# Window attention with an 8x8 Fourier product, then a merge layer: scores ahead of the forward transforms, inverse product ahead of P times V, softmax steps moved forward

## The reference, cut to what matters

```python
# layer 0: x = x + attention(groupnorm(x)), windows of 8x8 = 64 tokens, 6 heads of 32
o = irfft2(rfft2(q * SCALE) * rfft2(k))        # per channel, over the 8x8 window
attn = softmax(o @ v.T + bias)                 # 64 x 64 per window and head
y = attn @ v ;  x = x + y @ proj_w.T + proj_b
# layer 1: x = x + merge(g + laplacian(g)) with g = groupnorm(x)
edges = depthwise 3x3 [[0,-1,0],[-1,4,-1],[0,-1,0]] of g
x = x + 1x1 conv(g + edges, merge_w) + merge_b
```

## Time and profile before

| | before |
|---|---|
| median of 3 | 5582.83 us (5579.11 to 5585.63) |
| profiled execution | 5583.07 us, of which the span is 5581.1 us |
| granted TensorE clock, mean | 0.993 |
| PE busy | 5361.9 us (96%) |
| PEld busy | 4600.8 us (82%) |
| DVE busy | 4260.3 us (76%) |
| POOL busy | 4100.5 us (73%) |
| ACT busy | 3836.9 us (69%) |
| DMA | 99 GB/s mean |

### The profile page before, as it was taken

How to read it: one execution, slowest core, us unless ns; L and a number is a source line. 1 busy time by engine, 2 the same in 40 slices (tenths; PEclk the granted TensorE clock), 3 DMA queues, 4 the chain that set the end, 5 groups by cost and what they waited for, 6 DMA issues and landing times.

```text
span 5581.1 us, 208229 instructions
## 1 busy us (share of the span) xinstructions
PE 5361.9 (96%) x90620; PEld 4600.8 (82%) x90620; DVE 4260.3 (76%) x6658; ACT 3836.9 (69%) x7653; POOL 4100.5 (73%) x3518
## 2 busy tenths in 40 slices
PE   8999999999999999999999999999999999999988
PEld 5888888888888888888888888888888888888866
DVE  5777677777787777787777877787777777777757
ACT  3777776677766777667766677666776677776743
POOL 1555567788777787778777788777777778778774
PEclk9999999999999999999999999999999999999989
DMA  4222123333333233333333333333333332233336
GB/s 140 72 68 63 53 79 109 108 91 97 107 108 111 82 108 104 109 106 83 106 104 114 97 88 111 108 108 96 93 102 113 110 91 83 81 87 83 87 96 188
DMA packets 392509, 550.42 MB, mean 99 GB/s; under 512 B 24822, under 2 KB 284729, under 8 KB 391610
## 3 DMA queue, kind: packets, MB, share of 16 engines
q1 hardware_dynamic: 391612, 537.11, 33.5%
HBM read 335.69 MB, written 201.33 MB: 96 GB/s over the span
## 4 chain that ended last, share of the span: by engine, by line
PE 74%; DVE 18%; ACT 5%; issue 2%; POOL 1%; SPq 0%; DMA 0%; POOLq 0%; DVEq 0%; ACTq 0%
PE b_q L580 21%; PE b_t L613 6%; PE b_t L674 5%; PE b_s L692 5%; PE b_q L660 5%; PE b_s L528 4%; DVE xhl L962 4%; PE b_t L650 4%; PE b_s L530 4%; DVE probs L912 3%; DVE ssum L940 3%; DVE late L948 3%; PE b_s L541 3%; PE b_t L627 3%; ACT probs L1125 3%; PE b_s L539 2%
## 5 line engine op out<-in xcount | busy, mean ns | idle before, releaser
L1251 POOL TENSOR_TENSOR probs<-probs,srec 128x768 f32<-128x768 f32 x512 | 775.2, 1514 | 516.6 <-DVE srec L958 516.6
L1230 POOL TENSOR_TENSOR probs<-probs,smax 128x768 f32<-128x768 f32 x512 | 755.6, 1476 | 456.5 <-DVE smax L928 441.9
L906 DVE TENSOR_TENSOR qkl<-b_q,qkh 128x384 fp32r<-128x384 f32 x1024 | 569.6, 556 | 408.6 <-ACT qkh L975 407.3
L912 DVE TENSOR_TENSOR probs<-b_s,posb 128x768 f32<-128x768 f32 x512 | 490.2, 957 | 416.2 <-PE b_s L692 409.4
L940 DVE TENSOR_REDUCE ssum<-probs 128x12 f32<-128x768 f32 x512 | 488.0, 953 | 366.4 <-ACT probs L1125 366.2
L580 PE MATMUL b_q<-wnh,xh 128*128 128x288 f32 x2048 | 697.5, 341 | 61.4 <-DVE xhl L962 56.9
L975 ACT ACTIVATE qkh<-b_q 128x384 fp32r<-128x384 f32 x1024 | 503.1, 491 | 320.5 <-PE b_q L580 320.5
L975 ACT ACTIVATE probsT<-b_t 128x768 f32<-128x768 f32 x512 | 416.3, 813 | 367.8 <-PE b_t L613 367.8
L580 PE MATMUL b_q<-wnl,xhl 128*128 128x288 f32 x2048 | 606.1, 296 | 0.0
L1166 POOL TENSOR_TENSOR dg<-late 128x645 f32<-128x645 f32 x352 | 561.4, 1595 | 58.5 <-DMA late<-x_dram 35.3
L580 PE MATMUL b_q<-wnl,xh 128*128 128x288 f32 x2048 | 604.4, 295 | 0.0
(11 more groups left out here) (194 smaller groups left out, 15694.2 us busy)
## 6 DMA issues: line engine op xcount, KB each, us to landing
ld<-in_x SPq DMA_DIRECT2D x192, 512.0 KB, 4.6
late<-x_dram SPq DMA_DIRECT2D x112, 640.0 KB, 4.9
xs<-in_x SPq DMA_DIRECT2D x128, 512.0 KB, 4.0
x_dram<-late SPq DMA_DIRECT2D x128, 512.0 KB, 2.7
out<-late SPq DMA_DIRECT2D x128, 512.0 KB, 2.8
late<-x_dram SPq DMA_DIRECT2D x240, 192.0 KB, 5.5
xs<-in_x SPq DMA_DIRECT2D x128, 256.0 KB, 4.5
x_dram<-late SPq DMA_DIRECT2D x128, 256.0 KB, 3.5
```

The source lines that it names most:

```text
L906: V.tensor_tensor(qkl[:, i % 2, :], q_out, qkh[:, i % 2, :].bitcast(F32), ALU.subtract).then_inc(lo_out, 1)
L912: V.tensor_tensor(scored(i).rearrange("p (t q) m -> p t q m", q=4), scores.rearrange("p (t q m) -> p t q m", q=4, m=N), posb[:, :, :].unsq ...
L1230: P.tensor_tensor(probs[:, i % 2, :, :], probs[:, i % 2, :, :], smax[:, i % 2, :].unsqueeze(2).broadcast_to([128, 12, N]), ALU.subtract).t ...
L1251: P.tensor_tensor(probs[:, i % 2, :, :], probs[:, i % 2, :, :], srec[:, i % 2, :].unsqueeze(2).broadcast_to([128, 12, N]), ALU.mult).then_ ...
```

## The change

Numbers of lines in this section are those of the changed file where the rows of the order show them.

The diff, cut to what matters:

```diff
+EARLIER = 4
+        def closing(it):
+            img, at = divmod(it, 8 * NS)
+            return at + EARLIER * (img == B) if 1 <= img <= B else -1
 (m_task)
-            if at_blk == 1 and ph == 7 and 1 <= img <= B:
-                return ("mean", img - 1, 0)
-            if at_blk == 2 and 1 <= img <= B:
-                return (("dev", "mbias")[ph // 4], img - 1, 0)
+            if closing(it) in (15, 19, 23):
+                return (("mean", "dev", "mbias")[closing(it) // 4 - 3], img - 1, 0)
-        ALONE = PAIRS + 2 * 8
+        ALONE = PAIRS + 8
-        LATE = STRIPS - NS
+        LATE = STRIPS - NS - 1
 (sync)
-            for n in range(NLOAD):
-                stat_load(n)
             for dst, src in pos_loads:
                 sp.dma_start(dst, src).then_inc(pos_in, 16)
-            for dst, src in loads:
-                sp.dma_start(dst, src).then_inc(const_in, 16)
-            for n in range(NLOAD, NL):
+            for n in range(NL):
                 stat_load(n)
+                if n < len(loads):
+                    sp.dma_start(loads[n][0], loads[n][1]).then_inc(const_in, 16)
 (tensor, start)
-            pe.wait_ge(const_in, 16 * len(loads))
+                if b == 0:                       # in group_mean
+                    pe.wait_ge(const_in, 16 * len(loads))
-                if m == 38:
+                if m == 56:
                     group_mean(0)
-                elif m == 41:
+                elif m == 59:
                     group_spread(0)
-                elif m == 57:
-                    bias(0, 0)
-                if m == 61:
-                    pe.wait_ge(m_read, 3)
-                    bias(0, 1)
             last.then_inc(pos_mm, 1)
+            bias(0, 0)
+            bias(0, 1)
 (vector, last image's statistics)
+                    if u == STRIPS - 1:
+                        if ph == 0:
+                            dve.wait_ge(x1_done, (u + 1) * SD)
+                            for part in range(4):
+                                x1_stats(u, part).then_inc(g2_stats, 1)
+                            dve.wait_ge(g2_stats, 4 * B)
+                            for t, m in ((0, CA), (1, CB)):
+                                V.bn_aggr(...).then_inc(g2_mean, 1)
 (vector, loop: new order of a double)
                 s_out (pair 2)
+                smax (pair 2)
                 prod (pair 1); remainders(2 * j)
-                smax (pair 2)
                 statistics(2 * j)
+                ssum, then srec (pair 2)
                 m_result(2 * j); norms(2 * j); late stencil; remainders(2 * j + 1)
-                ssum (pair 2)
+                if j % 2 == 0: statistics(2 * j + 1)
                 x1 (pair 4)
-                srec (pair 2)
-                h = (j + 2) // 2
-                if j % 2 == 1: xhl
-                m_result(2 * j + 1)
+                m_result(2 * j + 1)
+                h = j // 2 + 1
+                if j % 2 == 0: xhl
+                if j % 2 == 1: statistics(2 * j + 1)
                 norms(2 * j + 1)
-                statistics(2 * j + 1)
 (scalar)
+                merge_weights(2 * j)     # mn, ahead of the exponential
+                exponential (pair 2), stood behind the copy of vT
 ...
+                centre; a_result(2 * j + 1)
+                merge_root(2 * j + 1)    # square root, right behind "dev"
+                osb, yT, yh, yb, then qh
 (gpsimd)
+                if closing(2 * j) == 20: newton(...)     # behind the subtraction
+                multiply by srec: ahead of xl and of the last stencil step
```

More of the change, by code:

```diff
@@ L299, in region_free, with bias_out @@
             m_wait(eng, last)
+        def bias_out(b, part):
+            return b_s[:, 0:QKV // 2] if b == 0 and part == 1 else b_s[:, 512:512 + QKV // 2]
         def m_wait(eng, it):
@@ L639, in _ @@
                 m_slot(2 * j + 1, pair)
+                if pair(1):
+                    pe.wait_ge(prod_done, pair(1)[1])
+                    if pair(0):
+                        pe.wait_ge(lo_out, 2 * j + 2)
+                    for k in range(6):
+                        for g in range(2):
+                            last = mm(o_out_ps[g * N:(g + 1) * N, k * N:(k + 1) * N],
+                                      prod[:, g * 6 + k, :, :].rearrange("p h d -> p (h d)"), inv[:, :],
+                                      start=True, stop=True)
+                    last.then_inc(o_mm, 1)
                 if pair(3):
@@ L653, in _ @@
                     last.then_inc(y_mm, 1)
[L654 to L676, removed]
                 if pair(1):
@@ L695, in _ @@
                     last.then_inc(s_mm, 1)
+                if pair(0):
+                    pe.wait_ge(lo_out, 2 * j + 2)
+                    for i in range(2):
+                        if i == 1 and pair(3):
+                            pe.wait_ge(yT_out, pair(3)[1])
+                        elif i == 1:
+                            pe.wait_ge(vT_out, pair(0)[1])
+                        for k, xx in enumerate((qkh, qkl)):
+                            for win in range(2):
+                                rows = slice(win * N, (win + 1) * N)
+                                last = mm(q_banks[0:NF, 2 * i + win, 0:QK], fwdh[rows, :], xx[rows, i, :],
+                                          start=(k == 0), stop=(k == 1))
+                    last.then_inc(t_mm, 1)
         @block.vector
@@ L795, in _ @@
             dve.wait_ge(const_in, 16 * len(loads))
+            group_parts(0)
+            group_dev(0, 1)
+            group_channels(2)
+            group_root()
+            scaled()
+            minus_mean()
+            dve.wait_ge(pos_mm, 1)
+            V.tensor_copy(posb[:, :, :], b_q[:, 0:N * 3].rearrange("p (m t) -> p t m", t=3)).then_inc(pos_done, 1)
+            rounded(0)
+            remainder(0)
             V.tensor_copy(fwdh[:, :], fwd)
@@ L924, in _ @@
                     remainders(2 * j)
+                statistics(2 * j)
                 if pair(2):
                     i, n = pair(2)
-                    dve.wait_ge(s_out, n)
-                    V.tensor_reduce(smax[:, i % 2, :], scored(i), AX.X, ALU.max).then_inc(max_done, 1)
-                statistics(2 * j)
+                    dve.wait_ge(exp_done, n)
+                    V.tensor_reduce(ssum[:, i % 2, :], scored(i), AX.X, ALU.add).then_inc(sum_done, 1)
+                    dve.wait_ge(sum_done, n)
+                    V.reciprocal(srec[:, i % 2, :], ssum[:, i % 2, :]).then_inc(rec_done, 1)
                 m_result(2 * j)
@@ L1110, in _ @@
                 split(h, 0 if j % 2 == 0 else 2)
+                merge_weights(2 * j)
+                if pair(2):
+                    i, n = pair(2)
+                    act.wait_ge(sub_done, n)
+                    pr = probs[:, i % 2, :, :].rearrange("p s m -> p (s m)")
+                    A.activation(pr, pr, ACT.Exp).then_inc(exp_done, 1)
                 if pair(3):
@@ L1128, in _ @@
                     border(blk - STENCIL_LAG)
+                if stencil_unit(j):
+                    centre(*stencil_unit(j))
                 a_result(2 * j + 1)
+                merge_root(2 * j + 1)
                 if j % 2 == 0:
                     split(h, 1)
+                if pair(1):
+                    act.wait_ge(o_mm, pair(1)[1])
+                    copy(osb[:, :, :].rearrange("p k n -> p (k n)"), o_out_ps).then_inc(o_out, 1)
                 if pair(3):
```

111 lines of the change are left out of this document (49 added, 62 removed).

## The result

| | before | changed |
|---|---|---|
| median | 5582.7 us (4 runs, 5579.11 to 5585.63) | 5697.94 us (4 runs, 5695.43 to 5703.12) |
| ratio | 1 | 1.0208 (95% interval 1.0190 to 1.0226) |
| profiled execution, span | 5583.07, 5581.1 us | 5695.43, 5693.3 us |
| granted clock, mean | 0.993 | 0.997 |

The account below looks back on a forecast made before the run. TensorE was taken as the bound (74% of the chain), waiting 0.6 us in a double for DVE's xhl. Terms +31 (doubles 72 to 511), +25 (0 to 71), -8 (start), -6 (last blocks) gave +42: 5625 us, range 5560 to 5690.

Parts of the forecast that it names:

- The turn: One round of the circle, y to y, in each double: 7.21 + 1.75 + 0.85 = 9.81 us, plus second merge slot.
- The two branches: Two ways from y to POOL's subtraction: 3.79 us through yb on POOL, 3.72 us through DVE's addition and maximum.
- the circle: Waits closing through four engines: y, yT, yh, yl, yb, subtraction, exponential, probsT, vs, transposes of v, o, y.
- The image's 12 us in 64 doubles: Estimate for an image's bias and small products, activation table changes and delays: 12 us, 0.19 per double (9 to 16).
- Doubles 0 to 71: Early doubles without merge slots: 9.526 us before, 9.88 after, +25 us in all (+19 to +33).
- Start and last blocks: Start: -8 us from position loads issued sooner; last blocks: -6 us from fewer slots and shared work.
- 9.33 + 0.47 is the turn again: Check of the turn: TensorE's own 9.33 us per double plus transposes of v coming 0.47 us late.
- rival 3: Circle turns slower: TensorE's own pauses, formerly partly hidden in xhl waits, add 0.14 us per double; 5697 us, chance 0.15.
- Rivals 1, 2, 4: Other outcomes: turn 9.72, 5576 us (0.15); POOL not late, 9.6, 5518 us (0.12); nothing new late, 5380 us (0.05).
- rival 1: Turn is 9.72 and start and tail give their best: 5576 us, no change; chance 0.15.
- Rival 4: Change does what it says, nothing new late, TensorE packed at 9.33 us per double: 5380 us; chance 0.05.
- The signs named: Expected in the changed profile: one-slot doubles at 9.8 us, POOL releasing the exponential, no xhl wait, first L580 about 75 us.

Follow-up runs that it names:

- e7: Changed kernel with POOL's yl and yb of a double behind the next double's subtraction instead of ahead of it: 5645.9 us.
- f15: Changed kernel with half of y (three of six heads of P times V) left out: 5610.62 us.
- e8: Changed kernel with the exponential over 384 of its 768 columns, leaving out half of the heads: 5565.37 us.
- e5: Changed kernel with the exponential on ACT, the sum and reciprocal on DVE and the multiplication on POOL all late: 5600.8 us.
- f14: Changed kernel with the first half of t between y and the scores on TensorE: 5883.94 us.
- e6: e5 with t between y and the scores on TensorE (o, y, t, scores): 5997.51 us.
- e12: Kernel before with the change's start and closing parts, and on DVE x1 and second merge result ahead of the sum, xhl one double sooner: 5448.41 us.
- e9: e5 with the first half of t between y and the scores, the second half behind the scores: 5670.74 us.

## Why the prediction was right or wrong

- *The turn.* Right, with some luck: of the 219 doubles with one slot in the main stretch 89 take 9.78 to 9.85, most often 9.80 or 9.81 (14 are shorter, down to 9.73; the others are longer), and those with two slots take 0.88 or 1.22 more (0.52 on the mean predicted, 0.525 measured). From yT to the transposes of v it is 6.45 us (2514.91 to 2521.36), as the terms say. The luck is in terms that were off and cancelled: the exponential holds ACT 0.85 us, not 0.74, and from probsT to the transposes it is 1.05, not 1.18; behind the transposes TensorE needs 1.81 us up to o, not 1.75, and from y to yT it is 0.69, not 0.76. The two branches were 0.13 apart, not 0.07 (e7). Of y's 0.76 only 0.06 could be saved, since o and osb end right behind it (f15).
- *The exponential ahead of probsT is on the circle.* Shown by e8, where the exponential's length came off the early doubles one for one, and by e5, where the same work in another order on ACT, DVE and POOL gives doubles of 9.31.
- *The image's 12 us in 64 doubles.* Of the 10.640 us mean of doubles 72 to 510, 9.81 + 0.525 are the plain ones. The rest, 0.305 x 439 = 134 us, are some 60 us of scores and t above their usual length and, by difference, some 74 us for 6.9 images, 10.8 each. Nearly all of it lies in about 24 of an image's 64 doubles, around the image's end and the next one's weights. The 12 was good. A piece of it is as foreseen, the root's table load ahead of osb and the next one ahead of the exponential, 1.28 us each:

```profile
1504.31 1.28 ACT L1086
...
1505.80 0.39 ACT osb L995
...
1510.64 1.28 ACT L1140
```

- *Doubles 0 to 71.* Turn right (9.72 to 9.83), sum 20 us short: 9.79 plain, 10.15 in the mean; over the 72 doubles the scores are 15.4 us above their usual length.
- *Start and last blocks.* -9.0 and -8.2 against -8 and -6; right.
- *Where it failed.* The step is the check "9.33 + 0.47 is the turn again" and the sum behind it: TensorE's groups in their new order stand there at the durations of the old one, and its own pauses, left to rival 3, are a term of zero. Measured, the scores alone are 73 us above their usual length in the changed kernel (57.3 in the main stretch and 15.4 in the first 72 doubles), and the profiled run is 70 us above the forecast. In the kernel before the scores are 21 us above their usual length, and these lie in its measured mean; so some 50 of the 73 are new.
- *Rival 3* had the term and its size (0.14 us in each double, 5697), but its reason covers at most those 21 us. It said that pauses which waits had hidden come to light. The runs show that the greater part comes of y and the scores standing back to back. By stops it is 19 before, 77 changed, 40 with half of t between (f14), 18 with half of y (f15), 0 with t between (e6); by the scores above their usual length 21, 73, 34, 16 and 4 us. On the circle nothing hides them, which is the part of rival 3 that was right.
- *Rivals 1, 2, 4* would have needed a turn of 9.72, 9.6 or 9.33. No double of the main stretch is under 9.73; a few of them, and 19 of the first 72, take 9.71 to 9.77, near rival 1's turn. Rival 4's 5380 was moreover out of reach, since TensorE's own work is 9.66 us in the fourth doubles (e12).
- *The signs named* came: exponential released by POOL (135.3 of its 135.9 us idle), subtraction behind yb, probsT behind the exponential, the transposes of v 4.80 us after the double's start (2516.56 to 2521.36), first L587 at 74.62. A wait for xhl is left only once, at the start.

What stays open: what decides when an instruction packet starts. At the stops of the changed kernel it started when TensorE was 118 to 230 records short of the place where it then stopped (median 179; before, 78 to 161, median 121), and TensorE goes on 2.2 to 2.9 us after that start. Why the number varies, no run shows. Whether e12's remaining stops (28, 10 us) can be had was not tried.

## What to carry to other kernels

When one engine's list is reordered, follow the circle through all the in-order engines, turn by turn, and add what each list puts ahead of a step; that gave 9.81, and 9.80 or 9.81 is the commonest turn. Then look at what now stands back to back: two groups of very small matmuls that other work used to separate can run out of instructions. And a move which frees one step can be worth its gain only if the list of the engine behind it is moved too: DVE's order alone brought 104 of the 134 us of e12, with TensorE and ACT left as they were.

## What the hardware showed that I had not expected

TensorE outruns the loading of its instructions. The 192 instructions of y and the scores take 1.5 us, 8 ns each, and o's 48 ahead of them 0.85; a packet brings 256, and TensorE goes on some 2.5 us after its start (medians of 2.5 to 2.8 in the runs). With 179 records left at the packet's start and 8 ns for each, that is 1.4 us of work in y and the scores (an estimate), about 1 us less than the packet needs; the stop shown above is 0.98. In the changed kernel all of these stops stand at one place of 256 records, as counted above, and in e5 too (117 of 117). Over the loop they sum to 48 us of 5695, with the short ones to some 73. The Trainium skill (Runtime: NRT & Kernel Launch, Instruction fetch mechanics) says that instruction fetch is hidden because the engine issues slower than its memory fills, and that a 16 KB block holds 256 instructions; the block agrees with 186,607 records in 729 packets, the hiding does not hold in this trace. A second point is the price of entering a group of products: t in two pieces took 0.54 + 0.54 us (f14 and e9), in one 0.89.
